# Windowed attention and a 3x3 convolution on one core: the q, k and v products in float16 parts, the output projection in a bank of its own

## The reference

```python
qkv = jnp.einsum('bchw,oc->bohw', x, W_qkv)          # 128 channels to 3*128
q, k, v = jnp.split(qkv, 3, axis=1)                   # q: windows of 8x8; k, v: windows of 12x12 around them
attn = jnp.einsum('bnd,bmd->bnm', q * SCALE, k)       # 4 heads of 32
attn = attn + rel_pos_emb(q, rel_height, rel_width) + FIXED_MASK
out = jnp.einsum('bnm,bmd->bnd', jax.nn.softmax(attn, axis=-1), v)
return jnp.einsum('bchw,oc->bohw', out, W_out)
```

## Time and profile before

| | |
|---|---|
| median of 3 runs | 4075.92 us (4075.8 to 4081.03) |
| the profiled execution's own time | 4075.55 us |
| its span, first to last instruction | 4073.7 us |
| mean granted TensorE clock | 0.992 of full speed |
| PE, DVE, ACT, POOL busy, share of the span | 92%, 83%, 70%, 52% |

### The profile page before, as it was taken

The page is one execution under the profiler, slowest core; times in us unless marked ns, Lnnn a source line. Parts: engine busy times, 40 slices in busy tenths (PEclk is TensorE's granted clock), DMA queues, the critical chain, the costliest instruction groups (busy, mean ns, idle before and its releaser), DMA issues. The chain is left out here.

```text
span 4073.7 us, 129480 instructions
## 1 busy us (share of the span) xinstructions
PE 3749.2 (92%) x48644; PEld 2632.9 (65%) x48644; DVE 3363.8 (83%) x5614; ACT 2831.7 (70%) x4805; POOL 2108.6 (52%) x2823
## 2 busy tenths in 40 slices
PE   0099999999999999999999999999958999999999
PEld 0077777777777777777777777777743444444444
DVE  9878888888888888888888888888878888888887
ACT  0077777777777777777777777777738777777774
POOL 0055555555555555555555555555527666666664
PEclk9999999999999999999999999999979999999999
DMA  9723323323323223223223223233224433344332
GB/s 400 293 67 93 91 77 93 90 78 93 88 80 93 85 83 93 83 84 93 82 86 93 81 87 93 77 90 93 68 69 162 152 149 153 151 154 151 154 145 93
DMA packets 490076, 462.47 MB, mean 114 GB/s; under 512 B 9408, under 2 KB 469056, under 8 KB 469184
## 3 DMA queue, kind: packets, MB, share of 16 engines
q1 hardware_dynamic: 489664, 455.92, 33.8%
HBM read 321.40 MB, written 134.48 MB: 112 GB/s over the span
## 5 line engine op out<-in xcount | busy, mean ns | idle before, releaser
L631 POOL TENSOR_TENSOR sb_erel<-sb_brel 128x288 f32<-128x288 f32 x512 | 351.0, 686 | 1018.6 <-DVE sb_brel L502 1018.4
L896 POOL TENSOR_TENSOR sb_tf<-sb_cf 128x1024 f32<-128x1024 f32 x256 | 609.3, 2381 | 393.7 <-DVE sb_tl L878 371.4
L401 PE MATMUL ps_t<-sb_ident,sb_d 128*108 128x128 f32 x4096 | 662.5, 284 | 1.7 <-ACT sb_pt L595 1.7
L421 PEld LDWEIGHTS ps_s<-sb_kf,sb_qb 128*64 128x64 f32 x16384 | 519.7, 138 | 182.2 <-issue 177.3
L535 DVE TENSOR_TENSOR sb_qb<-ps_q,sb_own_head 128x1024 f32<-128x1024 f32 x512 | 621.6, 1214 | 15.6 <-PE ps_q L386 15.6
L804 PE MATMUL ps_c<-sb_th,sb_wc_h 128*128 128x512 f16 x1536 | 584.9, 381 | 40.4 <-DVE sb_tl L878 40.4
L434 PEld LDWEIGHTS ps_v<-sb_wq,sb_zf 128*108 128x108 f32 x4096 | 511.3, 173 | 153.8 <-issue 81.4
L647 POOL TENSOR_TENSOR sb_prod<-sb_rel,sb_shift 128x192 f32<-128x192 f32 x1024 | 502.8, 512 | 198.7 <-DVE sb_rel L511 198.7
L421 PE MATMUL ps_s<-sb_kf,sb_qb 128*64 128x54 f32 x16384 | 586.1, 225 | 9.7 <-issue 6.5
L804 PE MATMUL ps_c<-sb_th,sb_wc_l 128*128 128x512 f16 x1536 | 583.9, 380 | 0.0
L804 PE MATMUL ps_c<-sb_tl,sb_wc_h 128*128 128x512 f16 x1536 | 583.8, 380 | 0.0
(11 more groups left out here) (94 smaller groups left out, 6453.2 us busy)
## 6 DMA issues: line engine op xcount, KB each, us to landing
sb_xb<-rows SPq DMA_DIRECT2D x128, 780.0 KB, 6.0
sb_xc<-x SPq DMA_DIRECT2D x64, 1280.0 KB, 5.4
sb_abuf<-rows SPq DMA_DIRECT2D x32, 2048.0 KB, 11.7
sb_x<-rows SPq DMA_DIRECT2D x128, 512.0 KB, 3.8
x<-sb_x SPq DMA_DIRECT2D x128, 512.0 KB, 4.1
out<-sb_oc SPq DMA_DIRECT2D x64, 1024.0 KB, 3.9
sb_raw<-wconv SPq DMA_DIRECT2D x1, 576.0 KB, 3.6
x<-sb_zrow SPq DMA_DIRECT2D x2, 128.0 KB, 2.1
```

What stands on the lines that cost most here:

```text
L401: last = pe.transpose(ps_t[0:KV, wj * 128:(wj + 1) * 128], d[:, at:at + KV], ident[:])
L421: last = pe.matmul(s_at, qb[:, qc:qc + QB], kf[:, kc:kc + KR], start=True, stop=True)
L631: pool.tensor_tensor(view(erel, 0, 128, 0, [[KN, PAIRS], [KS, KS], [1, KS]]), view(brel, 0, 128, 0, [[KS, PAIRS], [0, KS], [1, KS]]), view ...
L896: pool.tensor_tensor(tf[:, k * TF:(k + 1) * TF], view(cf, 0, 128, c0 + ra * W, [[2 * W, PAIRROWS], [1, W]]), view(cf, 0, 128, c0 + rb * W, ...
```

## The change

The parts of the diff, cut to their core:

```diff
-        wq = sb("wq", 3 * C, F32)
+        wq_h, wq_l = sb("wq_h", 3 * C, F16), sb("wq_l", 3 * C, F16)
-            zf = sb("zf", 4 * PAR * PLANE, F32, pb)
+            zf = sb("zf", 2 * PAR * PLANE, F32, pb)
+            zh, zl = sb("zh", 4 * PAR * PLANE, F16, pb), sb("zl", 4 * PAR * PLANE, F16, pb)
-            ps_o = ps("ps_o", 1024)
+            ps_o, ps_y = ps("ps_o"), ps("ps_y")
+            PRODUCTS = ((zh, wq_h), (zh, wq_l), (zl, wq_h))
 # PE, project
-                    need(pe, sem["x1_done"], n - 2 * GROUPS)
+                    pe.wait_ge(sem["zl_done"], piece + 1)
                     need(pe, sem["qb_done"], piece)
-                    pe.matmul(ps_q[:, 0:QP], wq[:, 0:C], z_at(slot, p, KS + 1, ...), start=True, stop=True)
+                    for c, (z, w) in enumerate(PRODUCTS):
+                        last = pe.matmul(ps_q[:, 0:QP], w[:, 0:C], z_at(z, slot, p, KS + 1, ...),
+                                         start=(c == 0), stop=(c == 2))
 # PE, o and y
-                            need(pe, sem["of_done"], m - 1)
+                            need(pe, sem["of_done"], m)
-                            need(pe, sem["qb_done"], QB_BEFORE(n))
                             need(pe, sem["x1_done"], n - 2 * GROUPS)
-                            pe.matmul(ps_q[:, 0:QP], wo[:], of[...])
+                            pe.matmul(ps_y[:, 0:QP], wo[:], of[...])
 # ACT, at the end of the body, after pt1
+                        if on(n - 1, GT):
+                            act.wait_ge(sem["sub_done"], n)
+                            act.activation(sp_[:, b1 * NS:(b1 + 1) * NS], ..., ACT.Exp, scale=alpha[:, 0:1])
+                        if g == 2 and on(u + 3, UNITS):
+                            edge_rows(u + 3, s + 1 + h, 1 - h)
+                        if g == 3 and on(u + 3, UNITS):
+                            own_rows(s + 1 + h, 1 - h, 0)
+                        if g == 0 and on(u + 2, UNITS):
+                            own_rows(s + 1, h, 1)
+                        if on(u + 2, UNITS):
+                            high(u + 2, slot, g)
+                    act.copy(z_at(zh, vslot + 2, p, 0, [[1, PLANE]]), view(zf, ...))     # high
 # POOL, at the end of the body
+                            pool.wait_ge(sem["zh_done"], v * PAR + p + 1)
+                            pool.tensor_tensor(z_at(zl, ...), view(zf, ...), z_at(zh, ...), ALU.subtract
+                                               ).then_inc(sem["zl_done"], 1)
```

More of the change, by code:

```diff
@@ L352, in body @@
                         row = settled(sp, (s + (h + 3) // 2) * WS)
-                        need(sp, sem["zf_done"], u + 2)
+                        need(sp, sem["zf_done"], 2 * (u + 2))
                         r = (slot + 3) % 2
@@ L433, in body @@
                             for p in range(PAR):
-                                last = pe.matmul(ps_v[0:KV, p * C:(p + 1) * C],
-                                                 z_at(vslot, p, GW * WK * vg, [[1, KV]]),
-                                                 wq[:, 2 * C:3 * C], start=True, stop=True)
+                                for c, (z, w) in enumerate(PRODUCTS):
+                                    last = pe.matmul(ps_v[0:KV, p * C:(p + 1) * C],
+                                                     z_at(z, vslot, p, GW * WK * vg, [[1, KV]]),
+                                                     w[:, 2 * C:3 * C], start=(c == 0), stop=(c == 2))
                             last.then_inc(sem["v_mm"], 1)
@@ L471, in _ @@
             def _(dve):
-                for slot in range(4):
+                for slot in range(2):
                     last = dve.memset(view(zf, 0, 128, slot * PAR * PLANE + (slot % 2) * (PJ - 1) * KS,
@@ L528, in body @@
                                               ).then_inc(sem["max_done"], 1)
+                        if g == 0 and on(u - 3, UNITS):
+                            dve.wait_ge(sem["x1_done"], (u - 2) * PAR)
+                            for c in range(2):
+                                dve.bn_stats(stats[:, bass.ds((u - 3) * 12 + c * 6, 6)],
+                                             x1[:, (1 - h) * WS * UW + c * 512:(1 - h) * WS * UW + (c + 1) * 512])
                         v, p, vh = (u + 1, g + 1, 1 - h) if g < 3 else (u + 2, 0, h)
@@ new lines, in body, with column, edge_rows @@
+                        if g == 0 and on(u + 2, UNITS):
+                            own_rows(s + 1, h, 1)
+                        if on(u + 2, UNITS):
+                            high(u + 2, slot, g)
+                def column(strip, part):
+                    return bass.ds(strip + part * STRIPS, 1)
+                def edge_rows(v, strip, vh):
+                    need(act, sem["zl_done"], (v - 1) * PAR)
+                    act.wait_ge(x_loaded[vh], (strip + 1) * 16)
+                    act.copy(aspare[:], bias[:])
+                    off = vh * PAR * PLANE + (1 - vh) * KS
+                    for part, row, ky in ((0, 0, 0), (2, ZR - PAD, KS - 1)):
+                        act.activation(view(zf, 0, 128, off + ky, [[2 * PLANE, 2], [PLANE, 2], [KS, LC // 2]]),
+                                       view(xb, 0, 128, (vh * ZR + row) * LC, [[LC, 2], [1, 2], [2, LC // 2]]),
+                                       ACT.Identity, bias=shift_t[:, column(strip, part)],
+                                       scale=rstd_t[:, column(strip, part)])
@@ new lines, in own_rows @@
+                def own_rows(strip, vh, py):
+                    off = vh * PAR * PLANE + (1 - vh) * KS
+                    act.activation(view(zf, 0, 128, off + 2 * py * PLANE + 1, [[PLANE, 2], [KS, LC // 2], [1, QS]]),
+                                   view(xb, 0, 128, (vh * ZR + PAD + py) * LC, [[1, 2], [2, LC // 2], [2 * LC, QS]]),
+                                   ACT.Identity, bias=shift_t[:, column(strip, 1)], scale=rstd_t[:, column(strip, 1)]
+                                   ).then_inc(sem["zf_done"], 1)
@@ L617, in _, with high @@
+                def high(v, vslot, p):
+                    if p == 0:
+                        need(act, sem["v_mm"], (v - 3) * GROUPS)
+                        act.wait_ge(sem["zf_done"], 2 * (v + 1))
+                    act.copy(z_at(zh, vslot + 2, p, 0, [[1, PLANE]]),
+                             view(zf, 0, 128, (vslot % 2) * PAR * PLANE + p * PLANE, [[1, PLANE]])
+                             ).then_inc(sem["zh_done"], 1)
                 act.wait_ge(sem["zeroed"], 1)
```

100 lines of the change are left out of this document (38 added, 62 removed).

## The result

| | before | after |
|---|---|---|
| median | 4076.81 us (4 runs) | 3851.01 us (3839.79 to 3859.64, 4 runs) |
| the profiled execution's own time | 4075.55 us | 3849.69 us |
| its span | 4073.7 us | 3847.9 us |
| mean granted TensorE clock | 0.992 | 0.983 |

The ratio is 0.9443, interval 0.9417 to 0.9468: 226 us faster. The forecast was 3740, with a range from 3705 to 3905: 336 us faster. So a third of the gain did not come, and the first question is where it went.

What follows compares the result with a forecast made beforehand. PE was taken to bound the attention, 5.23 of 5.444 us a group being its work; 0.49 less gives 4.74, plus 0.04 is 4.78. 511 steps save 339 us: 4075.6 - 339 + 3 = 3740 us, range 3705 to 3905.

Steps and rivals of the forecast that it cites:

- the forecast's own case: Whole kernel: groups of 4.71 to 4.86 us, 3705 to 3780 us in all; chance 0.62.
- rival 1: Attention on PE: v bound by its loads, a product every 80 ns, group 5.09 us, kernel 3898 us; chance 0.14.
- The loop's back edge: End of PE's attention loop: 0.04 us a group allowed for it together with odd waits that stay.
- q: PE's q matmuls in float16: 3 x 256 columns at 0.424 ns, 0.33 us a group, 0.11 less.
- k and v: PE's k and v matmuls in float16: k 0.50 us a group, 0.17 less; v 0.75, 0.21 less.
- the open term: PE's v, each product with its own load: 54 ns a product taken, bounds 54 and 108 ns.
- The waits: PE in attention: about 0.21 us a group of waiting goes, as q's wait for x1 and y's for qb vanish.
- Rival 2: Attention: waits stay or ACT makes new ones; 3827 us if 0.21 us a group stays, or 3790; chance 0.17.
- the 5.88 group: Attention's long group: blamed on DVE's body at g = 2, 6.0 us with both x1 passes, over PE's 5.23.
- ACT and POOL: New work in attention: ACT's cast 0.49 us, POOL's subtraction 0.92 us a group, neither delaying PE.
- Rival 3: POOL's mixed-type subtraction far slower; at four times the price 590 us more, 4670 us; chance 0.03.
- The start: Start of attention: first q also waits for cast and subtraction, ACT has more ahead; 3 us more.

Runs made afterwards that it cites:

- e1: The changed kernel with only PE's loop head placed at slot 0 of its 256-instruction block, closing branch at slot 230: 3755.07 us, ratio 0.9212.
- e2: The changed kernel with PE's loop head at slot 32, closing branch at slot 6: 3928.03 us.
- e3: The kernel before the change with PE's loop head at slot 200, closing branch at slot 6: 4301.63 us.
- e5: e1 with q's moving operand read as 256 float16 columns in a row, so q is of the wrong pixels: 3715.12 us.
- e11: e12 with DVE and ACT in the order of before, so nearly the float16 products alone: 4192.15 us.
- e7: e1 with the output projection y back in q's bank and its two waits back, new order kept: 4191.63 us.
- e12: e7 with PE's loop head at slot 216, closing branch at slot 222: 4151.91 us.
- e8: e1 with DVE's body in the order of before, y's own bank kept: 3756.68 us.
- e9: e1 with the exponential back at the head of ACT's body, for group n-2: 3811.58 us.
- e4: The changed kernel with eight units in a turn of the loop instead of four, code place left to chance: 3797.52 us.
- e6: e1 with one float32 product each for q, k and v; own bank, orders and ACT's and POOL's work kept; branch at slot 38: 4097.51 us.
- e10: e6 with PE's loop head at slot 200, closing branch at slot 238: 4036.13 us.

## Why the prediction was right or wrong

The direction was right, and the forecast itself was 111 us too fast. That the range held the time is luck: the forecast's own case ended at 3780, the range went on to 3905 for rival 1, which did not occur, and 3851 lies there because of a loss that no rival held. Its terms one by one:

- **The loop's back edge: the step that failed.** The prediction names no row for its "0.04 for the loop's back edge and odd waits that stay"; before, the edge costs 0.4 us a turn, 0.02 a group. It costs 3.45 us a turn, 0.19 a group, 97 us. It was taken as something that stays; it depends on where the code lies, and the change made PE's body 168 instructions longer. e1 (96 us gone with nothing but the place), e2 and e3 (made worse, in either kernel) show it. The mean granted clock, 0.983 against 0.992, was its first sign.
- **q: a mis-sized term.** 0.33 us from the convolution's rate, 0.41 measured, 0.08 x 511 = 41 us. The rate was right for k and for a q in a row (e5, 40 us), and not for runs of 4 float16 elements. In float32 the same runs cost nothing visible: 0.44 us for 256 columns is the rate of k.
- **k and v: right.** 0.50 and 0.76 us against 0.50 and 0.75. v was the open term, with 0.056 us a product at its lower bound. The load of 108 float16 columns takes 130 ns, 43 below float32's 173, close to the 42 that the prediction took for one pass; what a load is made of no run shows. It is over twice as long as the 56 ns from product to product, so loads run ahead of the products. The Trainium skill's figure (TensorE: Matmul & The Clock Gate, Back-to-back issue gap), 81 ns between products of 128 columns in a stream with loads, is not borne out here: 56 ns. It was rival 1, and did not occur.
- **The waits: right, and more than forecast.** 5.23 - 0.49 + 0.08 (q) = 4.82 is PE's own work, and e1 runs at 4.823 a group, so no odd wait stays and the rest of the 0.04 (20 us) was not needed. Rival 2 did not occur, since the bank and the orders take the waits away: without them it would have (e11, e7, e12, at up to 0.6 us a group). The cause given for the 5.88 group, both passes in one body of DVE, was not all of it: with an own bank that order does no harm (e8). It takes the shared bank as well to make a wait of a long body.
- **ACT and POOL: right.** Cast 0.523 us against 0.49, subtraction 0.939 against 0.92; neither reaches PE. Rival 3 did not occur. That the exponential's new place would matter was argued for only as harmless; it is worth 57 us (e9).
- **The start: wrong, small.** +3 us forecast, 1.4 less measured; the tail took 2.3 less.

The sum closes: 3740 + 97 (loop's end) + 41 (q) - 20 (allowance not used) - 4.4 (start) - 2.3 (tail) = 3851, against 3849.7 of the profiled execution.

That the code comes late can be read from the packets turn by turn. In each of the 28 turns of the kernel after a packet of code lands 0.7 to 3.2 us behind the start of PE's closing branch, and the branch ends 1.3 to 1.6 us behind that landing; the later the packet, the longer the branch (correlation 0.996). In e2, e3, e4, e6 and e7 the branch ends 1.2 to 1.6 us behind such a landing in every turn, and in e10 to e12 the cut S goes on 1.2 to 1.6 us behind one. Before and in e1, where the branch is cheap, the packet has landed 3.2 to 4.2 us ahead of the branch. The packets don't name their engine; it is this steady distance that ties them to PE's.

What stays open is why the packet is asked for when it is. The hint stands in the trace as an instruction of its own at the head of PE's body, 36 ns long and 77 to 79 us ahead of the branch (after), while the packet starts only near the branch, at a time that moves with the slots; what sets it off was not measured, nor was the slot read that the loop of the kernel after has by itself. The Trainium skill (Runtime: NRT & Kernel Launch, Instruction fetch mechanics) says that code comes in blocks of 256 instructions, and that a taken branch to a block outside the window must wait for it. The runs agree on the block (packets of e1 and e2, the cuts of S in e3, e10 and e11) and on the wait, and add what it leaves out: a branch at slot 222 to 238 cost 0.36 us, one at 6 to 38 from 3.9 to 4.8 (medians).

## What to carry to other kernels

When an edit changes the number of instructions in a hardware loop's body, look at the loop's end by itself: a stall with "issue" as its cause, once a turn, often followed by a lower granted clock, was here code that came late; see whether a packet of code lands just ahead of the end of each stall. The place of the loop's head moves it without touching the work. Take the worth of a change from the steady distance between like instructions and count the rare losses apart; e6 would have been misread by its time alone. And when one engine's work is shortened, free the shared buffer in the same change: here products alone brought 34 us, the bank and orders alone 114, both 317.

## What the runs showed of the hardware that was not expected

- The closing branch of a loop of 3047 instructions costs 0.36 us or 4.8 (median), by its slot; with the head at slot 200 or 216 a stall of 2.2 to 3.0 us on average begins 1.7 to 2.1 us behind the start of a cheap branch (e10 to e12).
- Where the branch waits, it ends 1.3 to 1.6 us behind the landing of a packet of 16,384 bytes of code, in each of the 28 turns of the kernel after.
- After 4.0 us without work PE was granted 0.50 of its clock for 6.8 us, so that the stall shown above cost 6.8 in all (S after 8.89 and 7.60 us instead of 4.83 twice). That is the worst turn; the mean stall of 2.44 us cost 3.45, and in 13 of 28 turns, with stalls of 1.6 to 2.6 us, the clock did not fall (in others as short it did).
- A float16 moving operand in runs of 4 elements takes 0.137 us for 256 columns, in a row 0.110 (e5). k's, 396 in a row, takes 0.167.
